# Eight experts for every token, or two per token on pages sorted by expert pair

## The chip, the cores and the metric

The kernel runs on one core of a Trainium2 chip. The core has five engines with instruction queues of their own: TensorE (PE in the profile; its weight loads are listed as PEld), VectorE (DVE), ScalarE (ACT), GpSimd (POOL) and SyncE (SP, which here only starts transfers). They meet only at semaphores. The metric is the time of one execution in microseconds on the device; the median of three runs of the kernel before is 1124.53 us.

## What is computed

The input x is 32 graphs of 256 nodes with 128 features, 8192 tokens in all. Four parts follow each other:

```python
x  = x + sum_over_5_node_groups(graph_conv(graph_conv(LN(x)[:, :25])))   # first 25 nodes only
x  = x + recurrence(LN(x))        # 256 steps in order: gates i, o, g; c = h*c + i*g; h = o*tanh(c)
x3 = x + (norm_adj + alpha*I) @ LN(x) @ W.T + b
# mixture of experts: E = 8, K = 2
xn = (x3 - mu) * rsqrt(var + eps) * gamma + beta
logits = xn @ Wr + br
top_vals, top_idx = top_k(logits, 2);  w = softmax(top_vals)
for e in range(8):                # W1[e]: 128 x 256, W2[e]: 256 x 128, exact gelu between them
    y += w_full[..., e:e+1] * (gelu(xn @ W1[e] + b1[e]) @ W2[e] + b2[e])
out = x3 + y
```

w_full is zero for the six experts that a token did not choose, so the reference needs only two of the eight.

## The kernel before

The program has three stages in time. **Setup** loads the inputs, runs the five small graph convolutions and ends with the first gate inputs of the recurrence (PE lines up to 573). **The recurrence** takes 256 steps in loops of four groups of eight steps. In a step TensorE does 15 small matmuls (line 594, vp stationary, h moving, 32 columns), ScalarE evacuates the gates (827, 829), VectorE runs a scan that makes the new c in the tile CC in SBUF (1111), ScalarE takes its tanh (831), and VectorE makes h in two halves of f16 (1113, 1116). Between these, each group fills in the transposed and scaled adjacency of one graph (835 to 845, 1076, 1090), the layer norms and the stores of x and y to memory.

**The expert stage** works on 16 blocks of 512 tokens (two graphs). For a block, TensorE aggregates (`aggregate`, 642) and projects (`project`, 650 and 653), VectorE adds the residual (1144) and takes statistics, the normed block is transposed (659), and the router finds the top two experts on VectorE (`route`) and turns their weights into rows. Then all eight experts run on the whole block: `layer1` (680) is 6 matmuls of 512 columns, three products per half of the hidden dimension, since each f32 operand is carried as an upper and a lower half; ScalarE applies gelu (891); TensorE spreads the expert's weight over the partitions (`weight_rows`, 687); VectorE multiplies (`weighted`, 1210), ScalarE and VectorE split the result into halves (871, 1214), and `layer2` (699) is again 6 matmuls of 512 columns into one bank. `layer2` runs three experts behind `layer1`, and the front of the next block is written into fixed places between the experts of this one. The order is the order of the code on each engine; nothing is scheduled otherwise. The loads and stores stand on the SP queue, two buffers each.

Of the kernel before, what the change touches and what calls it, by code (L numbers as in the profile page):

```python
# [19 lines left out]
F16 = mybir.dt.float16  # L20
U32 = mybir.dt.uint32
ALU = mybir.AluOpType
# [21 lines left out]
LAG = 3  # L44
NB2 = B // 2


# [4 lines left out]
C_IOTA = C_MASK + 2 * NP  # L52
C_ONES = C_IOTA + E
C_SELE = C_ONES + P
C_N = C_SELE + E * P
# [18 lines left out]
def build(nc, io):  # L74
    x_in, adj_in, out = io["x"], io["adj"], io["out"]

    with ExitStack() as ctx:
# [6 lines left out]
        def sem(name):  # L84
# [7 lines left out]

        const = sb("const", [P, C_N])
        ident = const[:, C_ID:C_ID + P]
        ones = const[:, C_ONES:C_ONES + P]
        iota8 = const[:, C_IOTA:C_IOTA + E]
        adjT = sb("adjT", [P, B, 2, T])
        w1hi, w1lo = sb("w1hi", [P, E, HID], F32R), sb("w1lo", [P, E, HID], F32R)
        w2hi, w2lo = sb("w2hi", [P, E, 2, D], F32R), sb("w2lo", [P, E, 2, D], F32R)
# [4 lines left out]
        NV = 2 * NG + NG + 2 + 2 * E  # L104
# [4 lines left out]
        eb1 = vcols[:, 3 * NG + 2:].rearrange("p (e c) -> p e c", c=2)  # L109
        b2p = sb("b2p", [3 * E, 3, D], BF16)  # L110
        brow = sb("brow", [3, 4, P], BF16)
        ones3 = sb("ones3", [3, 2 * P], BF16)
        sel_e = sb("sel_e", [3 * E, E, P], BF16)
        identb = sb("identb", [P, P], BF16)
# [3 lines left out]
        ld_x, ld_adj25, ld_const, ld_wa, ld_wb, ld_small, ld_lstm = (sem(n) for n in (  # L118
            "ld_x", "ld_adj25", "ld_const", "ld_wa", "ld_wb", "ld_small", "ld_lstm"))
# [3 lines left out]
        with ExitStack() as rec:  # L123
# [8 lines left out]
            CC = sb("CC", [P, B, 2], where=rec)  # L132
# [17 lines left out]
            wst = sb("wst", [P, E * HID], where=pre)  # L150
            w2st = sb("w2st", [P, E, 2, D], where=pre)
            gw = sb("gw", [P, D], where=pre)
# [3 lines left out]
            b2st, b2ra, b2rb = (sb(n, [3 * E, D], where=pre) for n in ("b2st", "b2ra", "b2rb"))  # L156
# [42 lines left out]
        def pair(name, shape, dt=F32):  # L199
            return [sb(f"{name}{i}", shape, dt) for i in range(2)]  # L200

        yr, x2r = pair("yr", [P, 2, 2 * D]), pair("x2r", [P, 2, 2 * D])
        hts = sb("hts", [P, 4 * P])
        x3 = pair("x3", [P, 2, 2, D])
        xh = sb("xh", [P, 4, D])
        xnT = sb("xnT", [P, 4 * P])
        xhi, xlo = pair("xhi", [P, 4 * P], F32R), pair("xlo", [P, 4 * P], F32R)
        st_m, mv_m, ve_m, rs_m = (sb(n, s) for n, s in (("st_m", [P, 4, 6]), ("mv_m", [P, 4, 2]), ("ve_m", [P, 4]), ("rs_m", [P, 4])))
        half4, eps4, tick_m = sb("half4", [P, 4]), sb("eps4", [P, 4]), sb("tick_m", [P, 1])
        lg, top = sb("lg", [P, 4, E]), sb("top", [P, 4, E])  # L210
        top_i = sb("top_i", [P, 4, E], U32)
        idx = sb("idx", [P, 4, 2])
        dif, th = sb("dif", [P, 4]), sb("th", [P, 4])
        w12 = sb("w12", [P, 4, 2])
        oneh, ohw = sb("oneh", [P, 4, 2, E]), sb("ohw", [P, 4, 2, E])
        wf, wra, wrb = sb("wf", [P, 4, E]), sb("wra", [P, 4, E]), sb("wrb", [P, 4, E])
        wp = sb("wp", [P, 4, 3, E], BF16)
        wT = pair("wT", [3 * E, 4 * P], BF16)
        Gl = pair("Gl", [P, 2, 4 * P])
        Gw = pair("Gw", [P, 2, 4 * P])  # L220
        ghi, glo = ([sb(f"{h}{i}", [P, 2, 4 * P], F32R) for i in range(4)] for h in ("ghi", "glo"))
        yTs = sb("yTs", [P, 4 * P])
        outb = pair("outb", [P, 2, 2, D])
# [7 lines left out]
         setup_ready, maps_ready, split_ready, state_ready, var_a, rstd_a, dgs_ready, dgr_ready, rstd_first, var_first, tiny_ready, whi_ready) = (sem(n) for n in (  # L231
# [3 lines left out]
            "fused_ready", "f_ps", "x1_ready", "pool_chain", "setup_ready", "maps_ready", "split_ready",  # L235
            "state_ready", "var_a", "rstd_a", "dgs_ready", "dgr_ready", "rstd_first", "var_first", "tiny_ready", "whi_ready"))
# [11 lines left out]
        (ht_ps, hts_ready, c_ps, x3_ready, m_stats, m_aggr, m_vareps, m_rstd, xh_ready, xhT_ps, xnT_ready, xhi_ready,  # L248
         xlo_ready, logits_ps, router_chain, dif_ready, th_ready, wp_ready, wT_ps, wT_ready, l1_ps, wbc_ps, gelu_ready,
         gw_ready, ghi_ready, glo_ready, l2_ps, yT_ready, yo_ps, out_ready, cd_const, x3_copied) = (sem(n) for n in (  # L250
            "ht_ps", "hts_ready", "c_ps", "x3_ready", "m_stats", "m_aggr", "m_vareps", "m_rstd", "xh_ready", "xhT_ps",
            "xnT_ready", "xhi_ready", "xlo_ready", "logits_ps", "router_chain", "dif_ready", "th_ready", "wp_ready",
            "wT_ps", "wT_ready", "l1_ps", "wbc_ps", "gelu_ready", "gw_ready", "ghi_ready", "glo_ready", "l2_ps",
            "yT_ready", "yo_ps", "out_ready", "cd_const", "x3_copied"))
        cd_loaded = [sem(f"cd_loaded{i}") for i in range(2)]
        out_stored = [sem(f"out_stored{i}") for i in range(2)]
# [18 lines left out]
        out_v = out.rearrange("b (c n) d -> n b c d", c=2)  # L275

        def iterations(eng, body):

            body(0, 0, 0)
            with eng.Fori(0, NB2 // 2 - 1) as it:  # L280
                body(it * 2 + 1, 1, it)
                body(it * 2 + 2, 0, it + 1)
            body(NB2 - 1, 1, NB2 // 2 - 1)

# [4 lines left out]
        def _(sp):  # L289
# [4 lines left out]
            sp.dma_start(const[:], io["consts"]).then_inc(ld_const, 16)  # L294
# [9 lines left out]
            for i in range(2):  # L304
                sp.dma_start(adjn[i][:], adj_v[:, i]).then_inc(adj_loaded[i], 16)

# [23 lines left out]
            def store(o, par):  # L330
                sp.wait_ge(out_ready, o + 1)
                sp.dma_start(out_v[:, bass.ds(o * 2, 2)], outb[par][:]).then_inc(out_stored[par], 16)

            def iteration(j, par, h):
                if not (isinstance(j, int) and j == NB2 - 1):
                    if not isinstance(j, int) or j + 2 < NB2:
                        sp.wait_ge(ht_ps, j + 1)
                        sp.wait_ge(x3_ready, j + 1)
                        load(j + 2, par)
                if not isinstance(j, int) or j > 0:  # L340
                    store(j - 1, 1 - par)
# [954 lines left out]
```

## Time and profile before

| | |
|---|---|
| median of 3 runs | 1124.53 us (1124.07 to 1125.74) |
| profiled execution | 1126.91 us, its span 1125.1 us |
| PE, DVE, ACT, POOL busy | 84%, 72%, 50%, 15% of the span |
| recurrence, from its first step to its last group's end | 93.5 to 568.1 us |
| expert stage, first matmul of `aggregate` to the end | 577.85 to 1125.1 us |

The profile page gives busy time, the chain of work that ended last, and groups of instructions by line. A busy share is an average over stages, so the stages are looked at by themselves. The granted clock is a share of 2.4 GHz: 1.00 is 2.4 GHz and 0.50 is 1.2 GHz.

### The profile page before, as it was taken

What the parts mean: (1) busy time and instruction counts of PE and PEld (TensorE: products, weight loads), DVE (VectorE), ACT (ScalarE), POOL (GpSimd) and SP (SyncE); (2) the same over time, 40 slices, a digit from 0 to 9 for tenths busy, and PEclk for the clock granted to TensorE, in tenths of its full rate; (3) what the DMA queues carried; (4) which work ended last, traced back from release to release, by engine and by line L of the source; (5) the groups of instructions that cost most, each with busy time, mean ns of one, the idle gap of its engine ahead of it and who ended that gap; (6) DMA issues with size and microseconds to landing.
All of it is one profiled execution on the core that took longest, in us unless ns stands there. A gap on an engine that the chain in (4) does not pass through costs nothing.

```text
span 1125.1 us, 21842 instructions
## 1 busy us (share of the span) xinstructions
PE 942.1 (84%) x6990; PEld 643.4 (57%) x6990; DVE 805.4 (72%) x2993; ACT 557.3 (50%) x1568; POOL 167.4 (15%) x309
## 2 busy tenths in 40 slices
PE   0976777777777777777747999999999999999998
PEld 0754444444444444444425776667677766776765
DVE  4355777777777777777735778877777888777785
ACT  1233444444444444444414666666666666666664
POOL 5501111111111111111111001111010111100000
PEclk9995555555555555555557999999999999999999
DMA  7900111011111111111020000000000000000000
GB/s 203 163 3 20 39 38 37 28 34 36 37 37 33 37 37 37 32 33 33 28 70 19 1 29 29 28 28 28 0 28 28 28 28 28 28 16 12 9 9 19
DMA packets 58323, 39.70 MB, mean 35 GB/s; under 512 B 4191, under 2 KB 57636, under 8 KB 58276
## 3 DMA queue, kind: packets, MB, share of 16 engines
q1 hardware_dynamic: 55971, 36.83, 12.3%
q0 software_dynamic: 656, 2.11, 0.6%
q10 hardware_dynamic: 1674, 0.49, 0.2%
q8 instruction: 11, 0.18, 0.1%
q14 instruction: 11, 0.09, 0.0%
HBM read 26.12 MB, written 13.30 MB: 35 GB/s over the span
## 4 chain that ended last, share of the span: by engine, by line
PE 53%; DVE 27%; ACT 12%; issue 6%; DMA 2%; POOL 0%; SPq 0%; DVEq 0%; POOLq 0%
PE pb L680 13%; PE pb L699 12%; PE pb L594 9%; DVE CC L1111 6%; ACT tanh_c L831 5%; DVE h L1113 4%; ACT S L827 4%; DVE glo L1214 3%; PE pb L626 3%; PE pb L642 3%; PE pb L687 3%; DVE Gw L1210 2%; DVE ys L1040 2%; ACT GC L829 2%; PE pb L653 2%
## 5 line engine op out<-in xcount | busy, mean ns | idle before, releaser
L594 PEld LDWEIGHTS pb<-h,vp 128*128 128x128 bf16 x3840 | 142.2, 106 | 214.0 <-DVE h L1113 211.5
L594 PE MATMUL pb<-h,vp 128*128 128x32 f16 x3840 | 170.3, 191 | 94.0 <-DVE h L1113 86.0
L891 ACT ACTIVATE Gl<-pb,vcols 128x512 f32<-128x512 f32 x256 | 162.3, 685 | 144.8 <-PE pb L680 144.8
L1210 DVE TENSOR_TENSOR Gw<-Gl,pb 128x1024 f32<-128x1024 f32 x128 | 155.8, 1217 | 103.1 <-PE pb L687 92.6
L1214 DVE TENSOR_TENSOR glo<-Gw,ghi 128x1024 fp32r<-128x1024 f32 x128 | 157.7, 1232 | 0.0
L827 ACT ACTIVATE S<-pb 128x64 f32<-128x64 f32 x256 | 58.2, 227 | 162.4 <-PE pb L594 162.4
L871 ACT ACTIVATE ghi<-Gw 128x1024 fp32r<-128x1024 f32 x128 | 135.1, 1055 | 1.7 <-DVE Gw L1210 1.7
L568 PE MATMUL pb<-xbuf,us 128*128 128x256 f32 x198 | 118.2, 703 | 0.6 <-ACT xbuf L813 0.6
L680 PE MATMUL pb<-xhi,w1hi 128*128 128x512 f32 x256 | 115.6, 452 | 0.0
L1111 DVE TENSOR_TENSOR_SCAN CC<-S,GC 128x64 f32<-128x64 f32 x256 | 74.4, 291 | 51.7 <-ACT GC L829 46.2
L831 ACT ACTIVATE tanh_c<-CC 128x32 f32<-128x32 f32 x256 | 59.0, 231 | 93.5 <-DVE CC L1111 93.5
L699 PE MATMUL pb<-ghi,w2hi 128*128 128x512 f32 x256 | 103.1, 403 | 0.9 <-DVE glo L1214 0.9
L1113 DVE SCALAR_TENSOR_TENSOR h<-S,tanh_c 128x32 f16<-128x32 f32 x256 | 49.3, 192 | 75.9 <-ACT tanh_c L831 75.9
L699 PE MATMUL pb<-glo,w2hi 128*128 128x512 f32 x256 | 101.8, 397 | 0.0
L699 PE MATMUL pb<-ghi,w2lo 128*128 128x512 f32 x256 | 101.6, 397 | 0.0
L680 PE MATMUL pb<-xhi,w1lo 128*128 128x512 f32 x256 | 101.5, 396 | 0.0
L680 PE MATMUL pb<-xlo,w1hi 128*128 128x512 f32 x256 | 100.4, 392 | 0.0
L680 PEld LDWEIGHTS pb<-xhi,w1hi 128*128 128x128 f32 x256 | 48.6, 190 | 21.5 <-issue 15.0
L699 PEld LDWEIGHTS pb<-ghi,w2hi 128*128 128x128 f32 x256 | 48.1, 188 | 19.0 <-issue 7.0
L1116 DVE TENSOR_TENSOR h<-hs,h 128x32 f16<-128x32 f32 x256 | 49.2, 192 | 8.9
L680 PEld LDWEIGHTS pb<-xlo,w1hi 128*128 128x128 f32 x256 | 48.5, 189 | 11.4
L699 PEld LDWEIGHTS pb<-glo,w2hi 128*128 128x128 f32 x256 | 48.2, 188 | 11.7
(223 smaller groups left out, 1470.1 us busy)
## 6 DMA issues: line engine op xcount, KB each, us to landing
adjn<-in_adj SPq DMA_DIRECT2D x32, 256.0 KB, 2.7
x_d<-x2s SPq DMA_DIRECT2D x33, 128.0 KB, 1.8
y_d<-ys SPq DMA_DIRECT2D x33, 128.0 KB, 1.8
yr<-y_d SPq DMA_DIRECT2D x16, 256.0 KB, 2.8
x2r<-x_d SPq DMA_DIRECT2D x16, 256.0 KB, 3.1
out<-outb SPq DMA_DIRECT2D x16, 256.0 KB, 2.3
X<-in_x SPq DMA_DIRECT2D x4, 912.0 KB, 17.5
aW<-in_L_gnn_W SPq DMA_DIRECT2D x2, 640.0 KB, 10.8
```

The lines of the kernel that those rows point to most:

```text
L568: mm(o, us[:, q, :], xbuf[:], start=(q != 1), stop=False, skip_group_check=True)
L594: return mm(o, vp[p][:, q, :], h[:], start=False, stop=True, skip_group_check=True)
L680: m = mm(H[e % 2][c][:], w[:, e, c * P:(c + 1) * P], x[par][:], start=(k == 0), stop=(k == 2))
L699: m = mm(yT_b[:], w[:, e, c, :], g[e % 4][:, c, :], start=False, stop=(e == E - 1 and k == 6), skip_group_check=True)
L827: av(S[:, :, :, 1], io_v[k][:, :, cols], ACT.Sigmoid, scale=1 / SC)
L831: av(tanh_c[:], CC[:, :, 1], ACT.Tanh).then_inc(tanh_ready, 1)
L871: av(ghi[e % 4][:], Gw[e % 2][:], ACT.Copy).then_inc(ghi_ready, 1)
L891: a = av(Gl[e % 2][:, c, :], PB[2 * (e % 2) + c][:], ACT.Gelu, bias=eb1[:, e, c:c + 1])
L1111: v.tensor_tensor_scan(scan_flat(CC[:]), scan_flat(S[:, 0]), scan_flat(GC[:]), 0.0, ALU.mult, ALU.add).then_inc(cell_ready, 1)
L1113: v.scalar_tensor_tensor(out=h1[:], in0=S[:, 1, :, 1], scalar=SC, in1=tanh_c[:], op0=ALU.mult, op1=ALU.mult).then_inc(h1_ready, 1)
L1210: v.tensor_tensor(Gw[e % 2][:], Gl[e % 2][:], bc(PB[5][:].unsqueeze(1), [P, 2, 4 * P]), ALU.mult).then_inc(gw_ready, 1)
L1214: v.tensor_tensor(glo[e % 4][:], Gw[e % 2][:], ghi[e % 4][:].bitcast(F32), ALU.subtract).then_inc(glo_ready, 1)
```

## The change

Setup and the recurrence keep their form. The weights of the experts are no longer loaded by the POOL queue at the start and split there; they are loaded once in setup for their squares (which give scale factors, powers of two) and again, an expert at a time, in the routing stage, where ScalarE and VectorE split them into two f16 halves (`split_upper`, `split_lower`). The tile CC moves from SBUF to PSUM. The table of constants is loaded in two parts. The first four groups of the recurrence carry a few extra matmuls and squares (`once`), and POOL's and SP's loops stay or are unrolled.

The expert stage falls into two. **Routing** goes over the 16 blocks two at a time (F from 0 to 7, 1024 tokens). Each token's pair of experts, one of 28, gets a code; a scan and two matmuls (`places`) rank the token among those with the same pair; and GpSimd writes its row of 260 words (x3, the normed row in two f16 halves, two weights, the token number) to that place of a DRAM tensor by an indirect transfer, 128 rows each, 64 in all. When all are counted, VectorE and one matmul make a table of 91 **pages** of 128 rows, each of a single pair (91 is the most that 8192 tokens in 28 pairs can need, and is fixed). **The page loop** is straight code, 91 times: SP reads an address and loads the page, TensorE transposes it, runs both experts' layers in f16 halves with 128 moving columns and register addresses into the weights, and VectorE adds the two weighted outputs to x3, after which GpSimd scatters 128 output rows by token number.

```diff
+PAIRS = [(a, b) for a in range(E) for b in range(a + 1, E)]
+REG = B * T + P
+PAGES = (B * T + NQ * (P - 1)) // P          # 91
-            CC = sb("CC", [P, B, 2], where=rec)
+        CC = PB[7][:, 0:2 * B].rearrange("p (b k) -> p b k", k=2)
...
 # SP
+            for t in range(PAGES):
+                if t % 4 == 0:
+                    n = min(4, PAGES - t)
+                    _, rows = nc.values_load_multi_w_load_instructions(
+                        row_i[0:1, t:t + n], engines=[mybir.EngineType.SP], ...)
+                if t >= XR:
+                    sp.wait_ge(out_ready, t - XR + 1)
+                sp.dma_start(Xp[t % XR][:], xs_d[bass.ds(rows[t % 4], P), :]).then_inc(page_loaded[t % XR], 16)
...
 # POOL
-            experts = [(wst[:].rearrange("p (e h) -> p e h", e=E), io["L1_ffn_W1"].rearrange("e d h -> d e h"))]
-            for dst, src in experts:
-                pool.dma_start(dst, src).then_inc(ld_wb, 16)
+            for F in range(NF):
+                send(F, 0)                    # 4 indirect transfers of 128 rows x 260 words
+                if F + 2 < NF:
+                    norm_scale(F + 2)
+                send(F, 1)
+            for t in range(PAGES):
+                pool.wait_ge(out_ready, t + 1)
+                pool.indirect_dma_start(out_rows, bass.IndirectOffsetOnAxis(out_i[t % 4][:, 0:1], 0), outb[t % 4][:], None,
+                                        bounds_check=B * T - 1, oob_is_err=False).then_inc(out_stored[t % 4], 16)
...
 # PE, routing
+            for F in range(NF):
+                if F:
+                    places(F - 1)             # waits for route(F - 1) on DVE
+                for u in range(2):
+                    normed_transpose(2 * F + u)
+                if F + 2 < NF:
+                    aggregate(2 * F + 4)
+                    aggregate(2 * F + 5)
+                logits(2 * F)
+                logits(2 * F + 1)
+                if F + 2 < NF:
+                    project(2 * F + 4)
+                    project(2 * F + 5)
...
 # PE, pages
+            def layer1(t):
+                pe.wait_ge(xT_ready, t + 1)
+                if t >= 2:
+                    pe.wait_ge(gelu_ready, t - 1)
+                mm(h[:]..., b1T[:], bc(sel1[:, bass.ds(vs, 4)].unsqueeze(2), [NK, 4, P]), start=True, ...)
+                for j, v in enumerate((va, vb)):
+                    for c in range(2):
+                        mm(o, w1[c][0][:, bass.ds(v, P)], x[:, 0:P], ...)
+                        mm(o, w1[c][0][:, bass.ds(v, P)], x[:, P:], ...)
+                        m = mm(o, w1[c][1][:, bass.ds(v, P)], x[:, 0:P], ...)
+            for t in range(PAGES):
+                if t + 1 < PAGES:
+                    page_transpose(t + 1)
+                layer1(t)
+                if t >= 2:
+                    layer2(t - 2)
+                if t + 1 < PAGES:
+                    addresses(t + 1)          # loads three values, four register operations
...
 # ACT, pages
+            for t in range(PAGES):
+                gelu(t)
+                if t + 1 < PAGES:
+                    page_evacuate(t + 1)
+                gelu_upper(t)
...
 # DVE, pages
+            for t in range(PAGES):
+                gelu_lower(t)
+                if t >= 2:
+                    combine(t - 2)            # two operations on 128 columns, one on 1 column
```

What stands on TensorE in a row, in the middle of the expert stage before (one expert; w1hi and w1lo are the halves of the first layer's weights, ghi and glo those of the gelu):

```order
L680 MATMUL pb0<-xhi0,w1hi 128x512 [waits gelu_ready]
L680 MATMUL pb0<-xhi0,w1lo 128x512
L680 MATMUL pb0<-xlo0,w1hi 128x512
L680 MATMUL pb1<-xhi0,w1hi 128x512
L680 MATMUL pb1<-xhi0,w1lo 128x512
L680 MATMUL pb1<-xlo0,w1hi 128x512
L699 MATMUL pb4<-ghi1,w2hi 128x512 [waits glo_ready]
```

and on TensorE in the page loop of the changed kernel (off_i is the table of addresses, Xp a page, w1_00 and w1_01 upper and lower halves of the weights for one half of the hidden dimension):

```order
L901 TENSOR_LOAD off_i
L911 ISA x2
L915 ISA
L916 ISA
L896 MATMUL pb4<-identh,Xp4 128x128 [waits xT_ready,page_loaded4]
L896 MATMUL pb4<-identh,Xp4 128x128
L926 MATMUL pb1<-sel1,b1T 128x512 [waits gelu_ready,xT_ready]
L931 MATMUL pb1<-xT0,w1_00 128x128
L932 MATMUL pb1<-xT0,w1_00 128x128
L933 MATMUL pb1<-xT0,w1_01 128x128
```

The matmuls of 512 columns per weight load have become matmuls of 128 columns, 12 for each layer of a page, and a load of addresses with its register operations stands ahead of each page. On TensorE in the routing stage of the changed kernel one turn of F is this (trih and onesh are a triangle and ones for the ranks, xh the normed tokens, yr the loaded y, wrg the router's weights):

```order
L850 MATMUL pb7<-oneh0,trih 128x224
L851 MATMUL pb7<-earlier0,onesh 128x224
L829 MATMUL pb4<-const,xh1 128x128 x4
L829 MATMUL pb5<-const,xh1 128x128 x4
L808 MATMUL pb0<-adjT,yr0 128x256 x4
L808 MATMUL pb1<-adjT,yr1 128x256 x4
L839 MATMUL pb6<-wrg,xnT0 128x8 x4
L839 MATMUL pb6<-wrg,xnT1 128x8 x4
L817 MATMUL pb2<-brow,ones3 128x512
L820 MATMUL pb2<-gnn_wT,hts0 128x128 x4
```

The front of the blocks, which stood between the matmuls of the experts before, now stands by itself, with nothing of the experts beside it. On VectorE a page is four instructions (ra, outb: the sum for one expert and for both; out_i: the token numbers for the store):

```order
L1514 SCALAR_TENSOR_TENSOR glo2<-Gl0,pw2,ghi2 128x512 [waits ghi_ready]
L1523 SCALAR_TENSOR_TENSOR ra0<-pb2,Xp0 128x128 [waits l2_ps]
L1524 TENSOR_SCALAR out_i0<-Xp0,valid 128x1
L1526 SCALAR_TENSOR_TENSOR outb0<-pb2,Xp0,ra0 128x128 [waits dve_chain]
L1514 SCALAR_TENSOR_TENSOR glo0<-Gl1,pw2,ghi0 128x512 [waits l2_ps,ghi_ready]
```

where two instructions of 1024 columns per expert and block (1210 and 1214) stood before.

## Rows read from the trace of the kernel before

**Rows 1.** Windows: start:end, length, busy time of each engine, clock, DMA share, GB/s

```profile
93.50:568.10 474.60, 360.95 (x4386) 230.51 (x4384) 341.76 (x1915) 203.00 (x1056) 83.70 (x190) 0.50 0.11 34
568.10:577.80 9.70, 0.69 (x2) 0.29 (x2) 2.31 (x14) 0.14 (x1) 1.82 (x6) 0.50 0.35 106
577.80:600.90 23.10, 11.97 (x44) 9.11 (x45) 7.62 (x43) 2.84 (x5) 2.38 (x7) 0.57 0.11 36
600.90:1125.10 524.20, 514.55 (x2310) 360.90 (x2308) 411.80 (x917) 331.58 (x476) 45.63 (x45) 0.99 0.07 21
```

**Rows 2.** Timeline of setup: start, length, instruction, idle before it and its releaser

```profile
11.77 1.46 DVE L924 BATCH_NORM_STATS2 st_a<-X 128x6 f32<-128x128 f32 x7 [11.77 <-DMA X<-in_x]
...
19.10 0.98 DVE L935 TENSOR_TENSOR adj<-adj,const 25x800 f32<-25x800 f32 x1 [0.48 <-DMA const<-in_consts]
```

**Rows 3.** Groups by line, recurrence: count, busy us, mean ns, idle before and releaser

```profile
L831 ACT ACTIVATE tanh_c<-CC 128x32 f32<-128x32 f32 x256 | 59.0, 231 | 93.5 <-DVE CC L1111 93.5
L829 ACT ACTIVATE GC<-pb 128x32 f32<-128x32 f32 x256 | 49.7, 194 | 0.0
...
DVE CC L1111 <- ACT GC L829: 46.2, 158, 4.9
```

**Rows 4.** Timeline, first block of the expert stage, clock mostly at 0.50

```profile
577.85 3.73 PE L642 MATMUL pb<-adjT,yr 128*128 128x256 f32 x8 [8.76 <-DMA x2r<-x_d]
...
588.90 1.12 PE L659 MATMUL pb<-const,xh 128*128 128x128 f32 x4 [5.48 <-DVE xh L1162]
...
590.88 1.87 PE L665 MATMUL pb<-wr,xnT 128*128 128x8 f32 x8 [0.87 <-ACT xnT L856]
...
592.79 0.19 DVE L1180 TENSOR_TENSOR lg<-pb,br 128x32 f32<-128x32 f32 x1 [0.57 <-PE pb L665]
...
596.41 0.60 PE L672 MATMUL pb<-identb,wp 128*24 128x128 bf16 x4 [3.65 <-DVE wp L1202]
```

**Rows 5.** Timeline in the expert stage at clock 1.00

```profile
864.37 0.38 PE L650 MATMUL pb<-brow,ones 3*128 3x128 bf16 x4
864.68 1.16 PE L653 MATMUL pb<-gnn_wT,hts 128*128 128x128 f32 x8
```

**Rows 6.** Chain of waits, one block's `aggregate` and one expert's layers at clock 1.00

```profile
891.94 1.92 PE pb L642 x8
893.87 1.40 PE pb L680 x6
895.26 1.40 PE pb L699 x6
```

**Rows 7.** Windows of the clock: columns as in rows 1

```profile
584.00:586.00 2.00, 0.00 (x0) 0.00 (x0) 1.47 (x11) 0.00 (x0) 0.22 (x2) 0.71 0.27 77
586.00:588.00 2.00, 0.00 (x0) 0.00 (x0) 0.98 (x2) 0.00 (x0) 2.00 (x2) 0.50 0.55 185
600.00:602.00 2.00, 2.00 (x6) 1.63 (x5) 0.00 (x0) 0.48 (x1) 0.00 (x0) 0.52 0.00 0
602.00:604.00 2.00, 2.00 (x13) 1.29 (x12) 0.00 (x0) 1.97 (x3) 0.00 (x0) 1.00 0.00 0
```

**Rows 8.** Groups by line, ACT and DVE: columns as in rows 3

```profile
L891 ACT ACTIVATE Gl<-pb,vcols 128x512 f32<-128x512 f32 x256 | 162.3, 685 | 144.8 <-PE pb L680 144.8
L813 ACT ACTIVATE xbuf<-pb 128x256 f32<-128x256 f32 x33 | 12.1, 366 | 7.5 <-PE pb L562 7.5
...
L1167 DVE TENSOR_TENSOR xlo<-xnT,xhi 128x512 fp32r<-128x512 f32 x16 | 10.9, 683 | 3.1 <-ACT xhi L857 3.1
...
L1076 DVE SCALAR_TENSOR_TENSOR adjn<-const,sdiag,adjn 128x128 f32<-128x128 f32 x64 | 22.1, 345 | 0.1
```

**Rows 9.** Groups by line, POOL: columns as in rows 3

```profile
L470 POOL TENSOR_TENSOR rs_m<-ve_m,half 128x4 f32<-128x4 f32 x16 | 16.1, 1009 | 1.2
...
L377 POOL DMA_DIRECT2D w2st<-in_L_ffn_W x2 | 1.8, 902 | 0.0
...
L377 POOL DMA_DIRECT2D wst<-in_L_ffn_W x1 | 1.2, 1177 | 0.5 <-issue 0.5
```

More of the change, by code:

```diff
@@ new lines, in _ @@
+            rows = None
+            for t in range(PAGES):
+                if t % 4 == 0:
+                    n = min(4, PAGES - t)
+                    _, rows = nc.values_load_multi_w_load_instructions(
+                        row_i[0:1, t:t + n], engines=[mybir.EngineType.SP], min_val=0, max_val=NQ * REG - P,
+                        skip_runtime_bounds_check_because="each row is the start of a region plus at most 8064 rows of its 8320")
+                if t >= XR:
+                    sp.wait_ge(out_ready, t - XR + 1)
+                sp.dma_start(Xp[t % XR][:], xs_d[bass.ds(rows[t % 4], P), :]).then_inc(page_loaded[t % XR], 16)
@@ L358, in _ @@
+            for i in range(4):
+                sp.wait_ge(out_stored[i], 16 * len(range(i, PAGES, 4)))
         @block.gpsimd
@@ L583, in _, with four_groups @@
             pe.wait_ge(state_ready, 3)
-            with pe.Fori(0, NGRP // 4) as it:
+            def four_groups(it, once):
                 for q4 in range(4):
@@ new lines, in addresses @@
+            def addresses(t):
+                _, (va, vb, vs) = nc.values_load_multi_w_load_instructions(
+                    off_i[0:1, t, 0:3], engines=[mybir.EngineType.PE], min_val=0, max_val=(E - 1) * P,
+                    skip_runtime_bounds_check_because="offsets of experts and of their selectors come from a table of constants")
+                offs[t] = va, vb, nc.s_assert_within(vs, 0, (E * E - 1) * 4,
+                                                   skip_runtime_bounds_check_because="the number of a pair out of 64, times the width of its selector")
+                lowered = nc.tensor.lower_ap
+                for v in (va, vb):
+                    for c in range(2):
+                        for k in range(2):
+                            lowered(w1[c][k][:, bass.ds(v, P)], for_matmul_weights=True)
+                for v in (va, vb):
+                    for c in range(2):
+                        for k in range(2):
+                            lowered(w2[c][k][:, bass.ds(v, P)])
+                lowered(sel1[:, bass.ds(offs[t][2], 4)])
+                lowered(bc(sel2[:, bass.ds(offs[t][2], 1)], [NK, P]), for_matmul_weights=True)
```

970 lines of the change are left out of this document (589 added, 381 removed).

## Prediction

> **What bounds the kernel now.** I read the windows by stage first. The recurrence is 474.6 us at a clock of 0.50 with no engine full; the expert stage from 600.9 us on is 524.2 us with PE busy for 514.55 of it, clock 0.99 [rows 1]. So the first stage is a chain of short waits and the last is bounded by TensorE. The chain of waits gives the price of the expert stage: at full clock one expert's `layer1` takes 1.40 us and its `layer2` 1.40 us, six matmuls of 512 columns each, and a block's `aggregate` 1.92 us [rows 6]. With 128 pairs of expert and block that is 128 x 2.80 = 358 us of the 547.3 us between 577.8 us and the end. The change goes at that part.
>
> **Columns.** Before, layers take 128 x 12 x 512 = 786,000 columns. Now 91 pages take 24 x 128 for the layers, 2 x 128 for transposes and 768 for biases, 4096 each, 373,000 in all. But a weight load now stands before each 128 columns, so columns alone don't give the price.
>
> **Setup, -5 us (0 to -7).** The first statistics wait 11.77 us for X, and the first step that needs the constants starts at 19.10 us [rows 2]. The weights (2 MB, POOL queue) and most of the constants no longer move in those microseconds. X can't land at once, and between the two rows lie 7.3 us of work that stay. I take 5. They come back later on SP's queue with 3.7 MB of zero rows, before the recurrence's first store; nothing waits for that queue there.
>
> **Recurrence, -3.5 us (-9.5 to +8).** CC in PSUM: tanh of 32 columns from SBUF is 231 ns, the same kind from PSUM 194 ns [rows 3], 37 ns x 256 = 9.5 us. It counts where the scan waits for ScalarE, 158 of 256 steps [rows 3]: 5.9 us. In the other steps VectorE's fill-ins are last. A write of VectorE to PSUM has no row; if it costs 37 ns more than one to SBUF, the gain is gone, and that plus a little is the upper end. The first 32 steps carry 16 small matmuls and 8 squares of 512 on ScalarE: I take 2.4 us for what sticks out. The Trainium skill ("ScalarE: Activation LUTs", the step-by-step part on what each stage is for) says that ScalarE is nearer to PSUM and VectorE nearer to SBUF: it gives the first half and warns of the second. By it alone the scan would take back what the tanh wins, and this term would be +2.4 us.
>
> **Handover, 0.** The store and reload between the stages (9.7 us, second row of [rows 1]) are as before.
>
> **The old expert stage goes: -547.3 us** (577.8 to 1125.1).
>
> **Routing, +166 us (130 to 215).** Here the front of the blocks has no experts beside it. One turn of F is a loop through PE, ACT and DVE: `places` waits for the last `route`, and the next `route` waits for what PE does behind it. At clock 0.50: two rank matmuls 0.5, transposes 2 x 1.12, aggregates 2 x 3.73, logits 2 x 1.87 [rows 4], three evacuations on ScalarE of about 0.65 (less than the 0.685 of gelu [rows 8]), `route`: for four tiles 592.79 to 596.41 us = 3.6 us [rows 4], for eight tiles without the splitting of weights but with the scan I take 4.6; semaphores 0.6. Sum 21 us. At full clock aggregates are 2 x 1.92 [rows 6] and the other PE pieces nearly halve: 14.8 us. The clock falls when PE idles (1.00 to 0.50 across 584 to 588 us, PE at 0.00) and comes back after a solid stretch (0.52 at 600 to 602, then 1.00) [rows 7], and each turn has both an idle stretch (`route`) and a solid one. So I take the middle, 17.5 us. VectorE's own work is no more: 7.62 us busy per block in the first front [rows 1], 15.2 for two. The sum: the first block's logits came 14.9 us after 577.85 [rows 4]; a second block, four aggregates ahead instead of one, doubled norms and GpSimd's new scale factors (some 25 small operations, at up to 1.009 us for a power [rows 9]) bring the end of the first `route` to +35 us. Then 5 x 17.5 = 87.5, two turns without aggregates 25. Then the count, the table (25 short VectorE operations, one matmul) and in parallel the last eight scatters, 11 to 14 us; the first page load and its transpose 4.5. Together 166.
>
> GpSimd must issue 8 scatters and about 2.4 us of powers per turn. No row shows an indirect transfer. The nearest, direct ones from POOL, took 0.902 and 1.177 us [rows 9]. At 1.2 us that is 12 us per turn, hidden; it decides from 1.9 us on.
>
> **Pages, +255 us (218 to 310).** PE at full clock: four pairs of bf16 weight load and matmul of 128 columns span 864.37 to 864.68 us, 0.078 us each [rows 5]. 24 x 0.078 = 1.87, two transposes 0.16, the biases 0.24 and 0.13 by 1.40/6 = 0.233 us per 512 columns [rows 6]: 2.40 us. To it comes the load of addresses and four register operations in PE's queue. No row has such a load. It costs nothing if the 12 matmuls of `layer2` ahead of it are still being worked off, and up to about 1 us if they are not; I take 0.4, so 2.8 us a page. The Trainium skill ("DMA: Bandwidth & Descriptors", latency and other measured facts) gives a floor of about 600 ns for such a load; fully exposed, with the operations behind it, the page would be an estimated 3.2 us and this term 291 us. The other engines: ScalarE 0.685 + 0.366 + about 0.71 = 1.76 us; VectorE 0.74 (0.683 and a pointer operand) + 2 x 0.345 + 0.2 = 1.65 us [rows 8]; GpSimd one scatter. The loop through ScalarE (`layer1` 1.2, gelu 0.69, evacuation 0.37, drain and semaphores 0.4) is 2.65 us, just under. 91 x 2.8 = 255. Six page buffers and four output buffers are three to four turns of 2.8 us, enough for transfers of some 2 to 5 us.
>
> **End, +7.5 us:** gelu, halves, `layer2`, combine, one scatter and its landing, of the last page.
>
> **Sum.** 1125.1 - 5 - 3.5 - 547.3 + 166 + 255 + 7.5 = 997.8 us span. The profiled execution took 1126.91 us and the median of the runs is 1124.53, 0.6 below the span, so about 997 us.
>
> **Rivals.**
> *The clock stays at 0.50 in the page loop (slower).* Four pairs of 128 columns took 0.60 us with their drain at 0.50 [rows 4], about 0.13 each: 24 x 0.13 + 0.26 + 0.7 + 0.4 = 4.5 us, 410 us for 91 pages, end at 1153 us. For it: 474.6 us of recurrence at 0.50 with PE busy by three quarters [rows 1]. Against it: there a burst has 15 matmuls of only 32 columns; here PE at 0.50 would be solid, and solid stretches went to 1.00 [rows 7]. It decides from a page of about 4.2 us on. Chance 0.08. A gap at each page may also flip the clock to and fro; that is in the next one.
> *Exposed addresses or a clock that flips.* 3.4 us a page, 309 us: 1052 us. For it: the load stands between the layers in PE's queue. Against it: PE's queue had no such idle in any row, but also no such load. Chance 0.20.
> *GpSimd's scatters bind routing.* At 2.5 us each a turn is 22.4 us and the last eight are 20: +45 us, 1042 us. For it: index rows are read and 128 rows addressed one by one. Against it: 1024 runs were issued in 0.902 us [rows 9]. Chance 0.14.
> *Everything hides.* Pages 2.5 us (228), turns 14.8 us (-14): 957 us. Chance 0.17.
> *Forecast*, within 25 us of 997: 0.40. 0.01 is left for no gain at all: so many pages and scatters that the halves cancel.
>
> **Numbers.** The likeliest case gives 997 us. The range of 935 to 1085 us reaches over the hidden case and both middle rivals, and leaves out the slow clock and combinations. What a measurement of this kernel can tell from no change is 0.2%, some 2.2 us; faster than that 0.90 (the four faster cases hold 0.91, of which 0.01 goes to a combination that ends slower), within 0.01, slower 0.09.
>
> **What would show it.** Right: PE clock at 0.9 or more in the page loop and about 2.8 us from one bias matmul of 512 columns to the next; page loop some 255 us; routing a little over 160 us with PE waiting for DVE in each turn; tanh_c near 194 ns. Wrong: PE idle before the transposes waiting for nothing but its queue by over 0.8 us; POOL busy over 90% in routing; ScalarE or a page load named as what PE waits for; a scan longer by over 37 ns than before.

## The result and the profile after

The changed kernel takes 1020.1 us (median of 4 runs, 1018.5 to 1020.97) against 1124.8 us in the same session; the ratio is 0.907, 95% interval 0.905 to 0.908. The forecast was 997 us. One run in the whole series, of e4 below (1029.4 us), lies over 1.5% above the fastest of its kernel and is left out of that kernel's times. The changed kernel's profiled execution has a span of 1019.2 us. These are its windows by stage (columns as in rows 1); they answer to [rows 1]. The stages are the recurrence, the handover, the routing, the page loop up to its last transposes and the end.

```profile
86.40:555.30 468.90, 368.78 (x4417) 234.57 (x4416) 341.88 (x1913) 198.94 (x1074) 84.58 (x195) 0.50 0.12 35
555.30:565.00 9.70, 1.69 (x6) 1.22 (x6) 2.65 (x16) 0.65 (x4) 1.77 (x4) 0.50 0.33 101
565.00:779.70 214.70, 114.67 (x483) 89.71 (x483) 93.34 (x521) 62.34 (x152) 105.98 (x144) 0.65 0.27 87
779.70:1002.50 222.80, 214.89 (x2506) 150.94 (x2507) 123.66 (x351) 142.87 (x272) 85.00 (x87) 0.97 0.27 74
1002.50:1019.20 16.70, 3.40 (x46) 2.46 (x43) 3.95 (x14) 1.41 (x2) 4.92 (x5) 0.72 0.01 0
```

In routing no engine is busy for more than 54% of the window. In the page loop PE is busy for 96% and the clock is 0.97. Stage by stage, in us of span:

| stage | forecast | measured | difference |
|---|---|---|---|
| setup, against 93.5 before | -5 | -7.1 | -2.1 |
| recurrence, against 474.6 | -3.5 | -5.7 | -2.2 |
| handover | 9.7 | 9.7 | 0 |
| routing | 166 | 214.7 | **+48.7** |
| pages and end | 262.5 | 239.5 | **-23** |

The differences add up to +21.4, which is 1019.2 less the forecast span of 997.8. So the total was near by luck: two large errors half cancelled, and neither stage came out as summed.

**The small stages.** The first statistics and the tanh and scan of the recurrence, as groups by line (columns as in rows 3):

```profile
L1176 DVE BATCH_NORM_STATS2 st_a<-X 128x6 f32<-128x128 f32 x7 | 1.5, 278 | 6.1 <-DMA X<-in_x 6.1
...
L1039 ACT ACTIVATE tanh_c<-pb 128x32 f32<-128x32 f32 x256 | 50.5, 197 | 95.3 <-DVE pb L1359 95.3
...
L1359 DVE TENSOR_TENSOR_SCAN pb<-S,GC 128x64 f32<-128x64 f32 x256 | 76.3, 298 | 55.0 <-ACT GC L1037 49.3
```

X is there at 6.1 us instead of 11.77 [rows 2]. The tanh takes 197 ns instead of 231 [rows 3].

**Routing.** The waits in 565 to 780 us (who waited for whom: us in total, times, longest):

```profile
DVE lg L1415 <- PE pb L839: 86.8, 7, 16.7
POOL xs_d L618 <- DVE slot L1446: 70.3, 6, 14.9
...
PE pb L808 <- DMA x2r<-x_d: 65.0, 7, 12.1
```

VectorE's router waits for the logits (839), GpSimd waits for VectorE's `slot`, and what they all stand behind is PE, whose `aggregate` (808) waits for the loads of the blocks. SP's own queue says what it waits for ahead of them (columns as above):

```profile
SPq L398 <- DVE w L1454: 141.7, 6, 25.1
```

Why the loads are late is in the timeline of one turn (start, length, instruction, idle before it):

```profile
653.86 0.68 DVE L1391 TENSOR_TENSOR stg<-pb,x2r 128x512 f32<-128x512 f32 x1
654.84 0.69 DVE L1391 TENSOR_TENSOR stg<-pb,x2r 128x512 f32<-128x512 f32 x1 [0.29 <-PE pb L820]
...
660.71 0.34 DVE L1454 SCALAR_TENSOR_TENSOR w<-wq,pw,w 128x128 f16<-128x128 f32 x1
661.08 0.34 SPq L398 DMA_DIRECT2D wq<-in_L_ffn_W  x1
661.46 0.47 SPq L399 DMA_DIRECT2D wq<-in_L_ffn_W  x1
662.03 0.41 SPq L394 DMA_DIRECT2D yr<-y_d  x1
...
663.54 0.47 SPq L395 DMA_DIRECT2D x2r<-x_d  x1
667.56 0.92 PEld L808 LDWEIGHTS pb<-adjT,yr 128*128 128x128 f32 x3 [11.83 <-DMA x2r<-x_d]
```

The buffers of the next block are free once the residuals have read them, from 654.5 us on. But on SP's queue the load of the next expert's weights (398) stands ahead, and it waits until VectorE has split the weights that lie in its buffer (`split_lower`, 1454, which ends at 661.05). So yr and x2r are issued at 662.03 us and later, they land some 4 us behind the last issue, and PE starts at 667.56. The wait names x2r; its cause is a buffer of weights that no one needs before the page loop. The late loads hold up the router only by a second matter of order: the logits of F stand behind the aggregates for F + 2 in PE's code, and their input, the evacuation of the transposed block (1101), behind that of the aggregates (1078) in ScalarE's. In this turn both evacuations of the aggregates came first, at 671.38 and 673.51 us, then 1101 at 674.01, although the transposes were done some 18 us before. No run put the logits first, so what that alone would give back is not known.

**The page loop.** PE's matmuls of one page (timeline):

```profile
849.00 0.27 PE L896 MATMUL pb<-identh,Xp 128*128 128x128 f16 x2
849.21 0.39 PE L926 MATMUL pb<-sel,b1T 48*128 x1
849.52 0.23 PE L931 MATMUL pb<-xT,w 128*128 128x128 f16 x1
849.59 0.22 PE L932 MATMUL pb<-xT,w 128*128 128x128 f16 x1
849.65 0.22 PE L933 MATMUL pb<-xT,w 128*128 128x128 f16 x1
...
850.15 0.22 PE L933 MATMUL pb<-xT,w 128*128 128x128 f16 x1
850.30 0.28 PE L944 MATMUL pb<-b2T,sel 48*128 48x256 bf16 x1
850.51 0.23 PE L948 MATMUL pb<-w,ghi 128*128 x1
...
851.14 0.22 PE L950 MATMUL pb<-w,glo 128*128 x1
851.39 0.27 PE L896 MATMUL pb<-identh,Xp 128*128 128x128 f16 x2
```

One page takes 2.39 us here. The twelve matmuls of a layer start 0.057 us apart (0.63 us over eleven steps), against the 0.078 us of [rows 5]. After the last one of `layer2` the next transposes come 0.25 us later instead of 0.06: that is the place of the load of addresses (e4 and e6 test it).

### The profile page after: what moved, and what is told of

Same layout as the page of the kernel before. It is cut to its first block, busy times and chain, and to the rows that moved or that the text cites. A ratio compares the mean times of both kernels' runs of the same rounds, so it can differ in the third digit from the quotient of the medians.

```text
span 1019.2 us, 23710 instructions
## 1 busy us (share of the span) xinstructions
PE 756.5 (74%) x7705; PEld 521.0 (51%) x7705; DVE 602.9 (59%) x2917; ACT 422.2 (41%) x1531; POOL 310.7 (30%) x492
## 4 chain that ended last, share of the span: by engine, by line
PE 39%; DVE 24%; ACT 16%; issue 12%; DMA 4%; POOL 3%; SPq 1%; ACTq 0%; POOLq 0%; DVEq 0%
PE pb L744 10%; DVE pb L1359 6%; ACT tanh_c L1039 4%; DVE h L1361 4%; PE pb L808 4%; ACT S L1035 4%; PE pb L776 4%; ACT xT L1140 3%; DMA x2r<-x_d 3%; PE pb L931 3%; PE pb L926 3%; PE pb L896 2%; PE pb L933 2%; PE pb L932 2%; DVE ys L1288 2%
## 5 line engine op out<-in xcount | busy, mean ns | idle before, releaser
L631 POOL DMA_INDIRECT out<-outb,out_i x91 | 89.9, 988 | 144.7 <-DVE outb L1526 138.1
L1514 DVE SCALAR_TENSOR_TENSOR glo<-Gl,pw,ghi 128x512 f16<-128x512 f32 x91 | 68.5, 753 | 106.5 <-ACT ghi L1152 106.5
L1359 DVE TENSOR_TENSOR_SCAN pb<-S,GC 128x64 f32<-128x64 f32 x256 | 76.3, 298 | 55.0 <-ACT GC L1037 49.3
L1146 ACT ACTIVATE Gl<-pb,pw 128x512 f32<-128x512 f32 x91 | 62.5, 687 | 79.8 <-PE pb L933 79.8
L618 POOL DMA_INDIRECT xs_d<-stg,slot x64 | 67.4, 1054 | 89.3 <-DVE slot L1446 70.3
L1039 ACT ACTIVATE tanh_c<-pb 128x32 f32<-128x32 f32 x256 | 50.5, 197 | 95.3 <-DVE pb L1359 95.3
L931 PE MATMUL pb<-xT,w 128*128 128x128 f16 x364 | 68.2, 225 | 0.0
L932 PE MATMUL pb<-xT,w 128*128 128x128 f16 x364 | 67.3, 222 | 0.0
L933 PE MATMUL pb<-xT,w 128*128 128x128 f16 x364 | 67.3, 222 | 0.0
L948 PE MATMUL pb<-w,ghi 128*128 x364 | 67.1, 223 | 0.0
L950 PE MATMUL pb<-w,glo 128*128 x364 | 66.2, 220 | 0.0
L949 PE MATMUL pb<-w,ghi 128*128 x364 | 66.2, 220 | 0.0
L1152 ACT ACTIVATE ghi<-Gl,pw 128x512 f16<-128x512 f32 x91 | 65.6, 721 | 0.0
## 6 DMA issues: line engine op xcount, KB each, us to landing
X<-in_x SPq DMA_DIRECT2D x4, 912.0 KB, 16.2
xs_d<-zrow SPq DMA_DIRECT2D x1, 3640.0 KB, 13.2
```

Source lines behind the costliest of these rows:

```text
L631: pool.indirect_dma_start(out_rows, bass.IndirectOffsetOnAxis(out_i[t % 4][:, 0:1], 0), outb[t % 4][:], None, bounds_check=B * T - 1, oob_ ...
L931: mm(o, w1[c][0][:, bass.ds(v, P)], x[:, 0:P], start=False, stop=False, skip_group_check=True)
L932: mm(o, w1[c][0][:, bass.ds(v, P)], x[:, P:], start=False, stop=False, skip_group_check=True)
L933: m = mm(o, w1[c][1][:, bass.ds(v, P)], x[:, 0:P], start=False, stop=True, skip_group_check=True)
L1039: av(tanh_c[:], CC[:, :, 1], ACT.Tanh).then_inc(tanh_ready, 1)
L1359: v.tensor_tensor_scan(scan_flat(CC), scan_flat(S[:, 0]), scan_flat(GC[:]), 0.0, ALU.mult, ALU.add).then_inc(cell_ready, 1)
```

## The experiments

Measured times stand beside the ratio to the kernel before of the same session, since that kernel's own median lay between 1124.8 and 1126.4 us. The changed kernel's ratio is 0.907.

**e1: the weights' loads wait for nothing.** Eight buffers, one per expert:

```diff
-        wq = ring("wq", 2, [P, 2, HID])
+        wq = ring("wq", E, [P, 2, HID])
 # SP
-                    if f >= 4:
-                        sp.wait_ge(wlo_ready, f // 2 - 1)
                     load_expert(f // 2)
```

> Eight buffers for the experts' raw weights instead of two, so that on SyncE's queue nothing waits for the low halves (wlo_ready) and the block loads behind them go when their buffers are free. Theory Q (the turn of routing is set by block loads queued behind the waiting weight loads, PE waits 65.0 us for them): routing 214.7 us falls by 25 to 45, to about 180; whole kernel about 985 us. Rival P (TensorE at the clock of 0.5 to 0.68 with its 26 us turn is the bound): under 3 us change, 1018 to 1021. Rival S (the scatters on GpSimd, 1.27 us apart, set the turns): change under 10 us, 1010 to 1020. The page loop must stay at 2.4 us per page by all of them.

Measured 972.8 us, ratio 0.865 (0.862 to 0.868). The gain of 47 us is a little more than theory Q's range and excludes both rivals. PE's wait for the loads fell from 65.0 to 17.5 us:

```profile
PE pb L807 <- DMA x2r<-x_d: 17.5, 8, 6.8
```

The first page's transposes start at 730.3 us instead of 779.7, so routing takes 165.3 us.

**e2: y and x2 with semaphores of their own**, on top of e1:

```diff
-                if f >= 2:
-                    sp.wait_ge(ht_ps, f - 1)
-                    sp.wait_ge(x3_ready, f - 1)
-                load(f, f % 2)
+                for f in (2 * F, 2 * F + 1):
+                    if f >= 2:
+                        sp.wait_ge(ht_ps, f - 1)
+                    load_y(f, f % 2)
+                for f in (2 * F, 2 * F + 1):
+                    if f >= 2:
+                        sp.wait_ge(x3_ready, f - 1)
+                    load_x(f, f % 2)
+                load_expert(F)
```

> As e1_weights_ahead, and y and x2 of a block have semaphores of their own; y is loaded as soon as the aggregate two blocks before has read its buffer, a turn earlier, and no longer waits for the residual. Theory Q: the landing of about 3 to 5 us still in the turn of e1 goes: routing falls by 15 to 20 us more, to about 165, the 17.5 us turn that the prediction took; whole kernel about 968 us. Rival P: same as e1. Rival S: same as e1 within 3 us.

Measured 960.1 us, ratio 0.852 (0.850 to 0.853). The direction is Q's, the size (12.8 us) is under its 15 to 20. PE now waits only once for the load of a block in the whole stage, 5.9 us before the first one, so the rest of the turns was no longer a matter of these loads. The edit changes two things together, the semaphores and the order of the loads; which of them gave how much is not shown.

**e3: the scale factors ahead of the scatters on GpSimd**, on top of e2:

```diff
-                send(F, 0)
                 if F + 2 < NF:
                     norm_scale(F + 2)
+                send(F, 0)
                 send(F, 1)
```

> As e2_own_semaphores, and on GpSimd norm_scale(F+2) stands ahead of the eight scatters of F instead of in their middle. If GpSimd binds the last turns (as the trace after reads, ScalarE waits 9.1 us for nb_m at 748.8): 5 to 9 us less than e2, and more than that if the turns have become short (rival S). If GpSimd is hidden: within 1 us of e2.

Measured 951.7 us, ratio 0.845 (0.843 to 0.846): 8.4 us less, within the expectation. With e5 below, which can't be told from it, this is the fastest version, 7% below the changed kernel. GpSimd's timeline of it shows what is left of a turn:

```profile
646.62 0.20 POOL L613 TENSOR_TENSOR nb_m<-nm_m,rs_m 128x8 f32<-128x8 f32 x1
647.43 1.09 POOL L623 DMA_INDIRECT xs_d<-stg,slot  x1 [0.60 <-issue]
648.82 0.98 POOL L623 DMA_INDIRECT xs_d<-stg,slot  x1 [0.30 <-issue]
...
655.21 1.70 POOL L623 DMA_INDIRECT xs_d<-stg,slot  x1 [0.30 <-issue]
657.22 0.96 POOL L623 DMA_INDIRECT xs_d<-stg,slot  x1 [0.31 <-issue]
658.26 0.24 POOL L610 TENSOR_SCALAR nm_m<-mv_m 128x8 f32<-128x8 f32 x1
658.56 0.20 POOL L611 TENSOR_SCALAR ve_m<-mv_m 128x8 f32<-128x8 f32 x1
658.84 1.67 POOL L612 TENSOR_TENSOR rs_m<-ve_m,half 128x8 f32<-128x8 f32 x1
660.59 0.20 POOL L613 TENSOR_TENSOR nb_m<-nm_m,rs_m 128x8 f32<-128x8 f32 x1
```

From one nb_m to the next are 13.97 us without a wait for another engine: by this trace the prediction's rival of GpSimd is true of this kernel, though it was not of the changed one. The next two experiments test that from both sides.

**e9 and e9b: more work for GpSimd, on either kernel.** Both get the same lines:

```diff
                 for i in range(half * NT // 2, (half + 1) * NT // 2):
                     pool.indirect_dma_start(...)
+                for _ in range(2):
+                    link(pw(spare[:], two8[:], half8[:], ALU.pow))
```

> e3_norm_first with four more powers of 1.7 us on GpSimd per turn, written to a tile that nobody reads: 32 of them, 54 to 58 us of GpSimd's time. Theory G (without the waits for loads GpSimd sets the turn of 13.9 us): nearly all of it shows, 45 to 56 us, 997 to 1008 us. Rival (VectorE, TensorE and ScalarE bind as much and GpSimd has slack): under 25 us more, below 977 us.

> The changed kernel with the same 32 powers on GpSimd. Theory Q (its turns of 27 us are set by loads queued behind the weight loads, GpSimd works 13.8 us of each): 6.9 us more in each turn is hidden in the first six and shows in the last two alone, 5 to 15 us in all, 1025 to 1035 us. Rival S (the scatters already bind there): 45 to 56 us more, 1065 to 1076 us.

On e3 it cost 56.3 us (1008.0; ratio 0.894), on the changed kernel 17.4 us (1037.5; ratio 0.922, 0.919 to 0.925). These are the last `slot` and the last scatter of the changed kernel (the first pair) and of e9b (the second); the last column but one gives first and last start:

```profile
L618 POOL DMA_INDIRECT xs_d<-stg,slot x64: 956/960/1692, 605.4 to 774.5; - x64
L1446 DVE TENSOR_REDUCE slot<-place x8: 542/544/550, 603.0 to 763.4; 128x8 uint32<-128x224 f32 x8
```

```profile
L620 POOL DMA_INDIRECT xs_d<-stg,slot x64: 956/961/1307, 603.8 to 788.3; - x64
L1450 DVE TENSOR_REDUCE slot<-place x8: 539/544/548, 602.4 to 764.2; 128x8 uint32<-128x224 f32 x8
```

The eight turns ended only 0.8 us later, so all the added work was hidden in them; the scatters that are left behind the last turn ended 13.8 us later. The expectation had the place right and its end (15 us) slightly low. In e9 the last `slot` moved by 37.1 us (689.7 to 726.8) and the last scatter by 55.4. So scatters were hidden in the changed kernel's turns, and in e3 GpSimd has next to no slack: of 54 to 58 us of added work 56.3 show.

**e5: less work for GpSimd**, on top of e3:

```diff
 # VectorE, statistics(F)
+                v.tensor_scalar(nm_m[F % 2][:], mv_m[F % 2][:, :, 0], -1.0, None, ALU.mult)
+                v.tensor_scalar(ve_m[F % 2][:], mv_m[F % 2][:, :, 1], LN_EPS, SC ** -2, ALU.add, ALU.mult).then_inc(m_aggr, 1)
 # GpSimd, norm_scale(F)
-                tp.tensor_scalar(nm_m[k][:], ...)
-                link(tp.tensor_scalar(ve_m[k][:], ...))
```

> As e3_norm_first, and the negated mean and the variance with its epsilon are computed on VectorE; GpSimd keeps the power and the product. Theory G (with the loads out of the way the queue of GpSimd is the bound of the turns: in e3 it does eight scatters at 1.27 us and 3.6 us of norm_scale per turn, 13.9 us, without a gap): each of some seven turns loses 0.5 to 0.8 us, routing 145 falls to about 140; 946 to 949 us. Rival V (VectorE or TensorE bind as well): no gain, or up to 1 us lost, 951 to 953 us.

Measured 951.4 us, ratio 0.845 (0.844 to 0.847): no difference that can be told from e3. In the trace the scatters run from 606.8 to 703.7 us, against 604.8 to 705.2: GpSimd's chain is 3.5 us shorter, but starts 2.0 us later: its first scatter comes 3.5 us after nb_m instead of 0.8, put down to issue, and why is open. The first page's transposes start at 709.0 us instead of 710.6. So theory G's number is missed and the time is the one that rival V named. That adding work costs (e9) and removing some gains nothing that can be measured shows that GpSimd binds in e3, but not by how much the next bound lies under it.

**e4: the addresses of page 0 for all pages.** The kernel leaves out which experts a page takes:

```diff
-                if t + 1 < PAGES:
-                    addresses(t + 1)
+                offs[t + 1] = offs[0]
```

> Leaves out which experts a page takes: the register loads and address operations of TensorE are done for page 0 alone and serve all 91 pages. Theory A (the load of 765 to 770 ns is hidden behind queued matmuls but for the idle time put down to issue, 18.8 + 16.5 us over the loop): 20 to 35 us less, a page at 2.05 to 2.2 us, 985 to 1000 us in all. Rival H (fully hidden, the issue gaps are the profile's own): within 3 us of 1020. Rival G (ScalarE's loop of gelu, upper half and evacuation, 1.8 us busy a page, takes over at once): less than 10 us gained.

Measured 1010.9, 1013.7 and 1021.5 us, ratio 0.899 (0.897 to 0.900): by the median 6 us less than the changed kernel, by the ratio 9, of the 20 to 35 us of theory A. These runs lie 1% apart, more than those of any other kernel here. In number that is rival G's range, but the trace, taken from the slowest of the three, shows another mechanism: pages run some 2.2 us apart for a while, and then PE stands still for a load. The microseconds around 841 (columns as in rows 1):

```profile
840.00:841.00 1.00, 0.03 (x1) 0.03 (x2) 1.00 (x4) 0.00 (x0) 0.80 (x1) 1.00 0.58 141
841.00:842.00 1.00, 1.00 (x12) 0.67 (x13) 0.25 (x1) 0.00 (x0) 0.00 (x0) 1.00 0.19 62
842.00:843.00 1.00, 1.00 (x11) 0.58 (x9) 0.00 (x0) 0.41 (x1) 0.96 (x1) 0.51 0.45 118
```

PE was idle for 1.8 us for a page load, and 1 us later the clock fell to 0.50 for about 3 us. Between 820 and 980 us it waited eight times for a page, 9.5 us in all, at a mean clock of 0.95. PE had become faster than six buffers of pages allow. The load in question landed after 3.9 us, where the median is 2.1.

**e6: the same with eight page buffers** (`XR = 8`), to take that stall away:

> As e4_addresses_once (leaves out which experts a page takes), and eight page buffers instead of six. In e4 the pages ran at 2.2 us apart until one page load that landed after 3.9 us instead of 2.1 stopped TensorE for 1.9 us, and then its clock was 0.50 for some 3 us. Theory A2 (the addresses cost 0.2 us a page, and e4 lost that to late page loads and the clock behind them): granted clock 1.00 through the loop, page at 2.2 us, 995 to 1004 us. Rival (the queue of loads itself cannot deliver a page in 2.2 us): as e4, 1010 to 1025 us with the clock at 0.95.

Measured 1001.7 us, ratio 0.889 (0.888 to 0.890): A2. The window from 820 to 980 us of the changed kernel, and of e6:

```profile
820.00:980.00 160.00, 155.50 (x1850) 109.46 (x1849) 92.53 (x264) 103.65 (x199) 64.82 (x66) 1.00 0.29 80
```

```profile
820.00:980.00 160.00, 160.00 (x2021) 118.43 (x2021) 100.80 (x288) 113.40 (x217) 71.93 (x72) 1.00 0.30 84
```

At 28 matmuls a page that is 66.1 and 72.2 pages, 2.42 and 2.22 us each. The addresses cost 0.2 us a page. These are the changed kernel's waits of PE's weight loads for its own queue in that window (columns as above):

```profile
PEld pb L931 <- issue: 14.9, 66, 0.2
PEld pb L896 <- issue: 13.1, 62, 0.3
```

The second, at the transposes, is gone in e6; the first, 0.2 us behind the bias matmul, stays in both and is no part of it. No run had eight buffers alone; they could have given the changed kernel little, since in this window its weight loads waited for pages for 0.9 us in all.

**e11: the register loads twice.**

> The changed kernel with the three register loads of each page done twice, the first set unused. Theory A2 (a set keeps TensorE's sequencer for a time of which the matmuls queued ahead hide all but 0.2 us): the second set is hidden by nothing, since the queue is empty by then; it shows in full, 0.6 to 1.1 us a page, 55 to 100 us, 1075 to 1120 us. Rival H (register loads are cheap, and the 0.2 us come from the address operations behind them): under 20 us more.

Measured 1020.0 us, ratio 0.905. It decides nothing. The trace holds 91 loads, not 182: the first set, which nothing used, isn't in the program that ran, so this is a second measurement of the changed kernel. What a second load costs is open.

**e10: the addresses of two pages in one load, and eight page buffers**, on top of e3:

```diff
-                _, (va, vb, vs) = nc.values_load_multi_w_load_instructions(off_i[0:1, t, 0:3], ...)
+                if t % 2 == 0:
+                    n = min(2, PAGES - t)
+                    _, vals[0] = nc.values_load_multi_w_load_instructions(off_i[0:1, t:t + n, :]..., ...)
+                va, vb, vs = vals[0][4 * (t % 2):4 * (t % 2) + 3]
```

> e3_norm_first with the offsets of two pages read by one set of register loads, and eight page buffers. Theory A2 (one register load of a page stops TensorE for 0.2 us): the page goes from 2.43 to between 2.22 (all of it) and 2.33 us (half): 9 to 18 us less than e3, 934 to 943 us. Rival (the gap goes with the number of registers loaded, not with the number of stops, and the loads come one behind another): no gain or a loss, 950 to 970 us.

Measured 956.3 us, ratio 0.849 (0.848 to 0.851): 4.6 us slower than e3, in the rival's range. The loads of the changed kernel (three registers) and of e10 (seven), min/median/max in ns, and e10's waits of PE's weight loads in 760 to 920 us:

```profile
L901 PEldq TENSOR_LOAD <-off_i x91: 765/770/1131, 773.0 to 1000.2; - x91
```

```profile
L908 PEldq TENSOR_LOAD <-off_i x46: 771/1073/1416, 696.9 to 934.1; - x46
```

```profile
PEld pb L901 <- issue: 17.1, 32, 0.7
```

One stop for seven registers leaves 0.53 us idle, two stops for three leave 2 x 0.21. A longer load may outlast the matmuls queued ahead of it, or the idle time may go with the number of registers; the two readings aren't told apart.

**e7: the raw weights back on GpSimd's queue at the start.** The changed kernel with one part undone:

```diff
 # SP
-            sp.dma_start(wst[:], ...).then_inc(ld_w, 16)
-            for c in range(2):
-                sp.dma_start(w2st[:, :, c, :], ...).then_inc(ld_w, 16)
 # GpSimd, behind its first three memsets
+            pool.dma_start(wst[:], ...).then_inc(ld_w, 16)
+            for c in range(2):
+                pool.dma_start(w2st[:, :, c, :], ...).then_inc(ld_w, 16)
```

> The changed kernel with one part undone: the three loads of 2 MB in all of the raw expert weights, wst and w2st, start on GpSimd's queue at the beginning, beside X, as before the change. Theory X (they took the bandwidth under X; their move is the gain of 7.1 us in setup): first statistics back from 6.1 to about 11.8 us, recurrence starts at 93.5, 1025 to 1028 us. Rival (the setup gained through other orders, adj or bias loads): within 2 us of 1020.

Measured 1028.2 us, ratio 0.912 (0.910 to 0.914). The first statistics wait 10.91 us for X, and the first scan of the recurrence starts at 92.9 us instead of 87.3: 5.6 of the 7.1 us are these loads. That is theory X; the other 1.5 us weren't looked into. The whole run is 8.1 us slower, and the 2.5 us that fall behind setup aren't explained either.

**e8: the cell state back in SBUF.**

```diff
+            CC = sb("CC", [P, B, 2], where=rec)
-        CC = PB[7][:, 0:2 * B].rearrange("p (b k) -> p b k", k=2)
```

> The changed kernel with one part undone: the cell state CC lies in SBUF again instead of PSUM. Theory C (ScalarE's tanh of the cell takes 231 ns from SBUF and 197 ns from PSUM, VectorE's scan 291 and 298, on a path walked 158 times): recurrence 468.9 us rises by 158 x 27 ns = 4.3 to 158 x 37 ns = 5.9 us, 1024 to 1027 us. Rival (latencies overlap, the 5.7 us came from the work beside the steps): within 1.5 us of 1020.

Measured 1025.3 us, ratio 0.910 (0.909 to 0.911). That is 5.2 us more by the medians, inside theory C. In the profiled run, the slowest of six (1030.1 us), 473.8 us lie between the first scan and the last instead of 467.5: 6.3 us, just over C's upper end. Its tanh and scan:

```profile
L1039 ACT ACTIVATE tanh_c<-CC 128x32 f32<-128x32 f32 x256 | 59.0, 231 | 93.4 <-DVE CC L1359 93.4
...
L1359 DVE TENSOR_TENSOR_SCAN CC<-S,GC 128x64 f32<-128x64 f32 x256 | 74.4, 291 | 53.7 <-ACT GC L1037 48.1
```

## Why the prediction was right, and where it was not

The total was near by luck, as said above; what follows goes term by term.

**Setup, right.** X was under the weight loads [rows 2]; e7 shows it with 5.6 us for a term of 5.

**Recurrence, right in mechanism.** tanh 197 ns for the 194 of [rows 3]; the unknown write of a scan to PSUM costs 7 ns more, not 37. e8 puts CC alone at 5.2 to 6.3 us. The count of 158 steps doesn't quite carry that: at 34 ns won and 7 lost they make 4.3 us, so either more steps than those gain, or a step gains more than the two lengths show; which is open. The term of 5.9 less 2.4 for the added matmuls and squares was too careful by those 2.4: they hardly show. The Trainium skill ("ScalarE: Activation LUTs", the step-by-step part) has VectorE nearer to SBUF; the trace agrees in sign, 298 against 291 ns, and at a fifth of what the tanh wins, so the term that this rule alone would have given (+2.4) was wrong.

**Handover, right**, 9.7 us.

**Routing, the step that failed** (+48.7 us). The prediction built the turn of F as "a loop through PE, ACT and DVE" and summed 14.8 to 21 us. It left SP out of that loop. The sign that it had named, PE waiting for DVE in each turn, did not come: ahead of the rank matmuls PE waited for VectorE 4 times, 7.9 us in all, and for loads 65.0 us. The queue of SP carries three kinds of loads in turn, and the change had put a new one, with a wait of its own, into it: the weights of the next expert, behind `split_lower`, ahead of the two loads that each `aggregate` needs. The logits of the eight turns came from 593.5 to 757.4 us, 23.4 us apart on average, with the aggregates of the last two missing. Without that wait the stage is 165.3 us (e1), with e2's own semaphores (for y a load a turn earlier) 154 us, and with e3 145 us, in which the logits of the turns come 13.2 us apart (591.4 to 683.8). So the sum over PE, ACT and DVE was even too high; what was missing was a queue. e1 alone gives back 47.3 us of the whole time, 49.4 us in the stage, against an error of 48.7. That e1 lands on the forecast's 166 us is again partly luck: it still waits 17.5 us for loads, and its turns are 16.2 us apart instead of 17.5.

**The clock of routing**, taken halfway, was 0.65; in e3, with shorter waits, it is 0.80 from 584 to 660 us. The middle was near enough; no run varied the clock by itself.

**Scatters, right for this kernel.** Taken at 1.2 us each, measured 0.96 us and 1.27 us apart. The rival with 2.5 us was wrong in its price. Its place is where e3 ended up: eight scatters at 1.27 us, one of them 0.7 us longer, and 3.1 us for `norm_scale` and the gaps beside it are the turn of 14.0 us. The prediction's limit of 1.9 us for a scatter held for a turn of 17.5 us; when the waits went, the turn fell and the limit with it.

**Pages, right in mechanism, too dear in two prices** (-23 us with the end). The layers were taken at 0.078 us per matmul of 128 columns from four matmuls [rows 5]; a long series with a weight load for each goes at 0.057: 22 steps x 0.021 = 0.46 us a page. The address load was taken at 0.4 us exposed and costs 0.2 (e6). Against these the biases, transposes and the gap behind the bias matmul take more than their columns, so that the page came to 2.42 us instead of 2.8. The first 10 us of the loop ran at a clock of 0.50, which the sum left out. The Trainium skill ("DMA: Bandwidth & Descriptors", latency and other measured facts) puts the floor of such a load at about 600 ns; this trace has 770 ns for three registers, of which 0.2 us is seen. The prediction's estimate of 291 us for a fully exposed load did not come. The end took 16.7 us from the last transposes, and had been taken at 7.5; part of that is the last page's own layers, which the sum counts with the pages. A term nobody varied is the number of pages: 8192 tokens would fill 64 of them, and the other 27 of the 91 cost an estimated 65 us at 2.42 us each.

**The clock in the page loop** stayed at 1.00 from 800 us on, against the rival of 0.50. e4 shows how thin the ground is: the page that kept PE waiting for 1.8 us also took the clock away for some 3 us, from 1 us after it.

## What to carry to other kernels

When you sum a loop, write down the queues that feed it as engines of their own, with what stands ahead of each transfer and what that waits for; a load that nobody needs soon, with a wait of its own, must not stand ahead of loads that the loop needs now. When such a wait goes, look at once for the next bound (here GpSimd's scatters), and test it by adding work to the suspected engine in both kernels. A test that adds work shows whether the engine has slack; it doesn't promise that taking work away pays (e5). Making the engine that binds faster gives less than its share when the ring of buffers before it was deep enough only for the old pace (e4 against e6).

## What the runs showed of the hardware

- f16 matmuls of 128 columns that each have a weight load of their own (98 ns, beside the previous matmul) start 0.055 to 0.057 us apart at clock 1.00.
- A load of three registers on PE's queue takes 770 ns, of seven 1073 ns (median), of four on SP's 301 ns. On PE's queue 0.21 us of the first and 0.53 us of the second show as idle time.
- An indirect transfer of 128 rows of 1040 bytes keeps GpSimd for 0.96 us, now and then for 1.7, with 0.30 us to the next; it lands after 2.6 us (median).
- A page load mostly lands after 2.1 us, but one took 3.9; with PE at 2.22 us a page six buffers didn't cover that. With eight, PE waited for no page between 820 and 980 us, but there the longest landing was 3.4 us.
